# Differential attention on one core: the maxima as rows by DMA, and both softmax sums multiplied before one transpose per quad

## The chip, the cores and the metric

The kernel runs on one core of one Trainium2 chip. The metric is the device time of one launch in microseconds (us); before the change it is 6063.33, the median of three runs (6057.4 to 6066.57).

## The reference

A sandwich of two sublayers on x of 16 batches x 1024 tokens x 256: `x = x + layernorm(attention(layernorm(x)))`, then the same with a mixture of experts. The change is in the attention:

```python
q = rope((x @ Wq).reshape(b, s, 32, 8)); k = rope((x @ Wk).reshape(b, s, 32, 8))   # 2 x 16 heads of width 8
v = (x @ Wv).reshape(b, s, 16, 16)
probs = softmax(q @ k.T * 8 ** -0.5)                 # 32 maps of 1024 x 1024 for each batch
w = probs[even] - lam * probs[odd]                   # the two maps of a head
attn = w @ v
attn = attn * rsqrt(mean(attn ** 2, -1) + 1e-5) * g  # over the 16 values of a head
```

Because the last line divides by the root mean square, attn may carry any factor for each token, if eps is multiplied by the factor's square. The kernel uses that instead of dividing by the softmax sums s1 and s2: with O1 and O2 the unnormalised sums of exp times v, it forms `O1 * s2 - lam * s1 * O2` and adds `(s1 * s2) ** 2 * eps` to the mean square.

## The kernel before

Five stages follow each other: `project` (q, k, v into scratch in device memory), `attend`, `route`, `experts`, `scatter`. Only `attend` changes.

`attend` works on quads: 4 of a batch's 32 maps (2 heads, each with its two maps c = 0 and c = 1). There are 128 quads, taken in a loop of 31 passes of 4 (`BUFS`) with the last 4 unrolled. A quad is 16 groups (`GROUPS`), 8 for each c, one for each tile of 128 keys.

- TensorE (PE), in program order: for each quad 64 `score` matmuls (line 766, keys x 512 queries, into three banks of `ps_e`), the `weighted_sums` of exp against v and 16 columns of ones (line 782, into `ps_o`, two groups late), and, for the next quad, 32 tries (`attempt`, line 795, two matmuls each, into two banks of `ps_m`). A try is one tile of 128 queries against all 1024 keys; it is there only to find the softmax maximum of each query.
- ScalarE (ACT): 64 exponentials for each quad (line 677). A score bank is reused when its exponential is done.
- VectorE (DVE): 32 maxima for each quad (`maximum`, line 691, 128 x 1024 each). Between them stand two 128x32 transposes of the maxima (`turn_maxima`, line 698), two 128x512 transposes of `ps_o` (`turn_sums`, line 703) and one 128x256 transpose of the result (`turn_out`, line 708). Their places are fixed: the transposes of sums stand in groups 1 and 9 (`LAG - 1`, `TILES + LAG - 1`), those of maxima in groups 0 and 8, `turn_out` in group 7 (`HEAD - 1`), each between the two maxima of its group.
- GpSimd (POOL): `split` writes minus the maxima as three bf16 parts (5 small instructions, twice for each quad); `finish` forms the result of a quad.
- SyncE (SP) issues every DMA of the stage in one order, `turn`: rows of maxima c = 0 of the next quad (`load_rows`: four stores to scratch, a wait for them, one load of three rows into `q_stack`, where they stand under the products, so that the score matmul subtracts the maximum), v, the rows c = 1, the 18 loads of the stacks four quads ahead (`load_stacks`, lines 59 and 65), and the four stores of the finished quad, which wait for `turn_out`.

Every engine works in its own order and waits on semaphores; the loop counters are in the wait values. PE waits at group 0 and at group 8 of a quad for the rows of c = 0 and c = 1, and a try waits until the maximum two tries back is done.

Of the kernel before, what the change touches and what calls it, by code (L numbers as in the profile page):

```python
# [22 lines left out]
F32 = mybir.dt.float32  # L23
# [5 lines left out]
P = 128  # L29
# [49 lines left out]
class Build:  # L79
    def __init__(self, nc, io, batches, ctx):  # L80
# [19 lines left out]
        self.max_scr = scratch("max_parts", (b * QKH // 2, PARTS, 2, S), BF16)  # L100
# [354 lines left out]
    def attend(self):  # L455
# [23 lines left out]
        PE_HEAD, ACT_HEAD, DVE_HEAD = 200, 160, 176  # L479
        with ExitStack() as ctx:  # L480
# [7 lines left out]
            v = sb("v", [P, BUFS, 2, 2 * VD * TILES])  # L488
            e = sb("e", [P, E_BUFS, HALF])
            largest, largest_t = sb("largest", [P, 2, 2, BLK]), sb("largest_t", [P, BLK])  # L490
            zeros, negated, rest = sb("zeros", [P, BLK]), sb("negated", [P, BLK]), sb("rest", [P, BLK])
            parts = sb("parts", [P, PARTS, BLK], BF16)
            sums_t = sb("sums_t", [P, 2, BLOCKS, BLK])
            scaled_s1, both = sb("scaled_s1", [P, BLOCKS]), sb("both", [P, BLOCKS])
            normed, attn_t = sb("normed", [P, 2, BLOCKS, VD]), sb("attn_t", [P, BLOCKS // 2, 2, VD])
# [11 lines left out]
            lam_done, lam_step, ones_set, largest_set = sem("lam_done"), sem("lam_step"), sem("ones_set"), sem("largest_set")  # L507
# [9 lines left out]
            ONES = 4  # L517
            SPLIT_STEPS, FINISH_STEPS = 4, 14
# [12 lines left out]
            def _(sp):  # L531
# [18 lines left out]
                def load_v(n, u):  # L550
                    sp.dma_start(v[:, u, :, 0:VD * TILES],
                                 self.v_scr[bass.ds(2 * n, 2)].rearrange("h p m -> p h m")).then_inc(v_loaded[u], 16)

# [32 lines left out]
            def _(pool):  # L586
                nc.gpsimd.memset(v[:, :, :, VD * TILES:], 1.0).then_inc(ones_set, 1)
# [5 lines left out]
                def split(h, base):  # L593

                    pool.wait_ge(max_turned, h + 1)
                    nc.gpsimd.tensor_tensor(negated[:], zeros[:], largest_t[:], ALU.subtract).then_inc(pool_step, 1)  # L596
                    if not (isinstance(h, int) and h == 0):
                        pool.wait_ge(max_stored, 16 * (P // BLK) * h)
# [8 lines left out]
                def finish(n, base):  # L607


                    s1, s2 = sums_t[:, 0, :, VD], sums_t[:, 1, :, VD]  # L610
                    pool.wait_ge(sums_read, 2 * n + 2 + 1)
                    nc.gpsimd.tensor_tensor(scaled_s1[:], s1, neg_lam[:].to_broadcast([P, BLOCKS]), ALU.mult).then_inc(
                        pool_step, 1)
                    nc.gpsimd.tensor_tensor(both[:], s1, s2, ALU.mult).then_inc(pool_step, 1)
                    nc.gpsimd.tensor_tensor(normed[:, 0], sums_t[:, 0, :, 0:VD], s2.unsqueeze(2).to_broadcast([P, BLOCKS, VD]),
                                            ALU.mult).then_inc(pool_step, 1)
                    pool.wait_ge(pool_step, base + 1)
                    nc.gpsimd.tensor_tensor(normed[:, 1], sums_t[:, 1, :, 0:VD],
                                            scaled_s1[:].unsqueeze(2).to_broadcast([P, BLOCKS, VD]),
                                            ALU.mult).then_inc(pool_step, 1)  # L620
                    pool.wait_ge(pool_step, base + 2)
                    nc.gpsimd.tensor_tensor(both[:], both[:], both[:], ALU.mult).then_inc(pool_step, 1)
                    pool.wait_ge(pool_step, base + 4)
                    nc.gpsimd.tensor_tensor(attn[:], normed[:, 0], normed[:, 1], ALU.add).then_inc(pool_step, 1)
                    pool.wait_ge(pool_step, base + 5)
                    nc.gpsimd.tensor_tensor(both[:], both[:], sixteen_eps[:], ALU.mult).then_inc(pool_step, 1)
                    pool.wait_ge(pool_step, base + 6)
                    nc.gpsimd.tensor_tensor(square[:], attn[:], attn[:], ALU.mult).then_inc(pool_step, 1)
                    step = 8
# [17 lines left out]
                def turn(n, rows, base):  # L647
                    if rows:
                        for c in range(2):
                            split(2 * (n + AHEAD) + c, base)  # L650
                            base = base + SPLIT_STEPS
                    finish(n, base)

                for h in range(2 * AHEAD):
                    split(h, SPLIT_STEPS * h)
                pool.wait_ge(lam_done, 1)
                start, steps = 2 * AHEAD * SPLIT_STEPS, 2 * SPLIT_STEPS + FINISH_STEPS
                with hinted(nc, pool, 0, loops) as i:
                    for u in range(BUFS):
                        turn(BUFS * i + u, True, start + steps * (BUFS * i + u))  # L660
                for u in range(BUFS):
                    n = BUFS * loops + u
                    turn(n, u < BUFS - AHEAD, start + steps * n - 2 * SPLIT_STEPS * max(0, u - (BUFS - AHEAD)))

            @block.scalar
            def _(act):
# [3 lines left out]
                with hinted(nc, act, 0, loops + 1, slot=ACT_HEAD) as i:  # L670
                    for u in range(BUFS):
                        n = BUFS * i + u
                        for j in range(HALVES):
                            act.wait_ge(scores_done, HALVES * n + j + 1)
                            if j % QUAD == 0:
                                act.wait_ge(sums_done, GROUPS * n + j // QUAD + 1 - E_GROUPS + E_GROUPS)
                            nc.scalar.activation(e[:, j % E_BUFS], ps_e[:, bank(u, j)], ACT.Exp,  # L677
                                                 scale=SCALE).then_inc(exp_done, 1)

            @block.vector  # L680
            def _(dve):
                nc.vector.memset(largest[:], 0.0).then_inc(largest_set, 1)
                dve.wait_ge(largest_set, 1)
                dve.sem_inc(max_done, 2)
                dve.sem_inc(sums_read, 1)
# [891 lines left out]
```

## Time and profile before

| | before |
|---|---|
| runs, us | 6066.57, 6057.4, 6063.33 |
| profiled execution, us | 6064.04 |
| its span, first to last instruction, us | 6062.2 |
| mean granted TensorE clock | 0.97 of 2.4 GHz |

Durations come from the profiled execution. Its page gives each engine's busy time; a timeline gives instructions in order, with rows of the same line merged and counted; an instruction's duration includes latency that overlaps its successor, so the cost of one in a dense row is the distance of two starts. `attend` fills some 4900 of the 6062 us, from 500 to 5435 us.

### The profile page before, as it was taken

To read this page: it belongs to the slowest core of one execution; us is meant where nothing else is said; L and a number is where in the kernel's file an instruction comes from. 1 tells how busy PE (TensorE), PEld (TensorE's weight loads), DVE (VectorE), ACT (ScalarE), POOL (GpSimd) and SP (SyncE) were. 2 spreads that over 40 slices of the span, in tenths; PEclk is the share of its full clock that TensorE was granted. 3 is DMA by queue.
4 is the path that set the end of the run, shared out by engine and by line. 5 is a ranking of instruction groups with operands and counts; after the bars stand their busy time and mean duration, and the time that the engine had idled before them with its cause. 6 is when DMAs were issued, how large, how long until landed. Compare 5 with 4: busy or idle time off the path is not lost. (4 is left out here: it accounts for less than half of the span.)

```text
span 6062.2 us, 166095 instructions
## 1 busy us (share of the span) xinstructions
PE 5630.7 (93%) x50896; PEld 2015.1 (33%) x50896; DVE 5537.9 (91%) x6200; ACT 4845.1 (80%) x8950; POOL 2006.0 (33%) x3781
## 2 busy tenths in 40 slices
PE   8878999999999999999999999999999999987775
PEld 4542233333333333333333333333233323325424
DVE  7868999999999999999999999999999999967706
ACT  5755888888888888889888888888888888873304
POOL 7981222222222222222222222222222222225406
PEclk9997999999999999999999999999999999998877
DMA  5672222222232222222222222222222222216598
GB/s 178 203 202 49 49 52 52 51 52 52 52 52 51 52 51 52 51 50 52 52 47 51 52 51 48 51 51 51 50 52 52 52 52 51 52 35 199 173 359 272
DMA packets 436840, 493.13 MB, mean 81 GB/s; under 512 B 99283, under 2 KB 298099, under 8 KB 436195
## 3 DMA queue, kind: packets, MB, share of 16 engines
q1 hardware_dynamic: 435171, 483.57, 32.7%
q8 instruction: 457, 7.49, 0.5%
q14 instruction: 188, 1.54, 0.1%
q10 hardware_dynamic: 1024, 0.53, 0.0%
HBM read 360.60 MB, written 123.21 MB: 80 GB/s over the span
## 5 line engine op out<-in xcount | busy, mean ns | idle before, releaser
L677 ACT ACTIVATE at_e<-at_ps_e 128x512 f32<-128x512 f32 x8192 | 4368.8, 595 | 542.5 <-PE at_ps_e L766 373.2
L691 DVE TENSOR_REDUCE at_largest<-at_ps_m 128x1 f32<-128x1024 f32 x4096 | 4671.1, 1202 | 56.2 <-PE at_ps_m L795 53.0
L782 PE MATMUL at_ps_o<-at_e,at_v 128*32 128x256 f32 (+1 forms) x30720 | 2687.1, 422 | 12.3 <-issue 8.2
L795 PE MATMUL at_ps_m<-k_stack,q_stack 48*128 48x512 bf16 x8192 | 2500.1, 385 | 132.7 <-DVE at_largest L691 58.3
L766 PE MATMUL at_ps_e<-q_stack,k_stack 51*128 51x512 bf16 x8192 | 2505.7, 383 | 5.2 <-issue 2.3
L782 PEld LDWEIGHTS at_ps_o<-at_e,at_v 128*32 128x32 f32 x30720 | 845.0, 149 | 1567.3 <-issue 935.0
L766 PEld LDWEIGHTS at_ps_e<-q_stack,k_stack 51*128 51x128 bf16 x8192 | 598.1, 93 | 1678.3 <-ACT at_e L677 1641.0
L596 POOL TENSOR_TENSOR at_negated<-at_zeros,at_largest_t 128x32 f32<-128x32 f32 x256 | 64.7, 253 | 3262.7 <-DVE at_largest_t L698 3262.7
L795 PEld LDWEIGHTS at_ps_m<-k_stack,q_stack 48*128 48x128 bf16 x8192 | 607.6, 93 | 203.5 <-DVE at_largest L691 172.2
L639 POOL TENSOR_TENSOR at_rms<-at_mean_eps,at_minus_half 128x16 f32<-128x16 f32 x128 | 372.7, 2912 | 10.0
L436 PE MATMUL pr_ps_q<-pr_xn_t,pr_w 128*128 128x512 f32 x512 | 232.3, 596 | 2.0 <-issue 1.3
L703 DVE STREAM_TRANSPOSE at_sums_t<-at_ps_o 128x512 f32<-128x512 f32 x256 | 179.2, 700 | 26.3 <-PE at_ps_o L782 26.3
L1040 ACT ACTIVATE ro_x<-ro_ps_y,ro_y_bias,ro_y_rstd 128x256 f32<-128x256 f32 x128 | 61.9, 564 | 165.4 <-POOL ro_y_bias L1002 165.4
L322 ACT CAST pr_parts<-pr_rotated 128x1024 bf16<-128x1024 f32 x64 | 66.8, 1044 | 136.1 <-POOL pr_rotated L266 112.2
L266 POOL TENSOR_TENSOR pr_rotated<-pr_rotated,pr_from_odd 128x1024 f32<-128x1024 f32 x64 | 166.0, 2594 | 29.0 <-DVE pr_from_odd L397 29.0
L633 POOL TENSOR_TENSOR at_square<-at_square 128x128 f32<-128x128 f32 (+3 forms) x512 | 158.7, 310 | 40.1
L271 POOL TENSOR_TENSOR pr_parts<-pr_rest,pr_parts 128x1024 bf16<-128x1024 f32 x64 | 163.4, 2554 | 13.2 <-ACT pr_parts L326 13.2
L382 DVE TENSOR_TENSOR pr_rest<-pr_rotated,pr_parts 128x1024 f32<-128x1024 f32 x64 | 135.0, 2109 | 35.8 <-POOL pr_parts L271 18.6
L1161 PE MATMUL ro_ps_y<-ro_wo,ro_attn 128*128 128x256 f32 x512 | 119.4, 390 | 28.8 <-DMA ro_attn<-attention 20.6
L436 PEld LDWEIGHTS pr_ps_q<-pr_xn_t,pr_w 128*128 128x128 f32 x512 | 98.0, 192 | 98.8 <-issue 94.4
L446 PE MATMUL pr_ps_v<-pr_w,pr_xn_t 128*128 128x256 f32 x512 | 123.4, 385 | 3.8 <-ACT pr_v_out L341 3.8
L1475 ACT ACTIVATE sc_out<-sc_ps,sc_bias,sc_rstd 128x256 f32<-128x256 f32 x128 | 61.7, 563 | 68.0 <-POOL sc_bias L1448 68.0
(130 smaller groups left out, 2856.0 us busy)
## 6 DMA issues: line engine op xcount, KB each, us to landing
k_stack<-k_parts SPq DMA_DIRECT2D x1536, 64.0 KB
q_stack<-q_parts SPq DMA_DIRECT2D x256, 192.0 KB
q_stack<-q_parts SPq DMA_DIRECT2D x256, 128.0 KB
w_first<-in_w SPq DMA_DIRECT2D x32, 1024.0 KB, 11.7
ex_w_second<-in_w SPq DMA_DIRECT2D x32, 1024.0 KB, 12.7
q_parts<-pr_parts SPq DMA_DIRECT2D x96, 256.0 KB, 2.4
k_parts<-pr_parts SPq DMA_DIRECT2D x96, 256.0 KB, 2.8
pr_x_in<-in_x SPq DMA_DIRECT2D x16, 1024.0 KB, 5.8
```

The lines of the kernel that those rows point to most:

```text
L266: nc.gpsimd.tensor_tensor(out, out, from_odd[:, ch % 2], ALU.add if ch % 2 else ALU.subtract).then_inc(add_done, 1)
L271: nc.gpsimd.tensor_tensor(parts[:, ch, 2], rest[:, ch % 2], parts[:, ch, 1], ALU.subtract).then_inc(part3_done, 1)
L382: nc.vector.tensor_tensor(rest[:, ch % 2], rotated[:, ch // 2, ch % 2], parts[:, ch, 0], ALU.subtract).then_inc(rest_done, 1)
L436: last = nc.tensor.matmul(ps_q[:, ch % 2, half * HALF:(half + 1) * HALF], w[:, k, ch // KC, cols], xn_t[:, u, k, half * HALF:(half + 1) * ...
L633: nc.gpsimd.tensor_tensor(square[:, :, 0:width], square[:, :, 0:width], square[:, :, width:2 * width], ALU.add).then_inc(pool_step, 1)
L639: nc.gpsimd.tensor_tensor(rms[:], mean_eps[:], minus_half[:], ALU.pow).then_inc(pool_step, 1)
L677: nc.scalar.activation(e[:, j % E_BUFS], ps_e[:, bank(u, j)], ACT.Exp, scale=SCALE).then_inc(exp_done, 1)
L691: nc.vector.reduce_max(largest[:, u % 2, j // SIDE, j % SIDE:j % SIDE + 1], ps_m[:, j % 2], AX.X).then_inc(max_done, 1)
L703: nc.vector.transpose(sums_t[:, c].rearrange("p b d -> p (b d)"), ps_o[:]).then_inc(sums_read, 1)
L766: nc.tensor.matmul(ps_e[:, bank(u, j)], k_stack[rows, u, pair, c, kt * P:(kt + 1) * P], q_stack[rows, u, pair, c, half * HALF:(half + 1) * ...
L782: last = nc.tensor.matmul(ps_o[32 * tile:32 * tile + 32, columns], v[:, u, tile // 2, kt::TILES], e[:, (QUAD * g + tile) % E_BUFS, columns ...
L795: last = nc.tensor.matmul(ps_m[:, j % 2, half * HALF:(half + 1) * HALF], q_stack[rows, u, pair, c, t * P:(t + 1) * P], k_stack[rows, u, pa ...
```

## The change

1. The maxima (`largest`, [128 queries, 16]) go to scratch as they are, in one DMA (line 549 of the changed kernel), and come back as `largest_t` [16 rows, 128 queries] in a second, element by element (line 554). DVE's two 128x32 transposes are gone. `split` works on 16x128 instead of 128x32. The three parts then go into `q_stack` in six DMAs, one row each (line 559).
2. `ps_o` is copied to `sums` by ACT, once for each c (`copy_sums`), and no longer transposed by DVE. v has ones on both sides, so that for c = 0 a map's rows are O1 | s1 and for c = 1 s2 | O2. POOL multiplies both copies (128x512), which gives O1*s2 | s1*O2.
3. For s1*s2, SP moves one row of sums of each map into `totals`, four DMAs for each c (`move_totals`, line 572), and POOL multiplies these too (128x32).
4. DVE transposes both products at once (128x544, line 746), in group 5 of the next quad (`TURN_SUMS`); `turn_out` moves from group 7 to group 11 (`TURN_OUT`). `finish` has 3 instructions fewer after it.

```diff
+            TURNS_BEFORE = 4
+            ROW_DMAS = PARTS * PAIR
+            DVE_HEAD_PERIODS, TURN_SUMS, TURN_OUT = 12, 5, 11
+            COPY_AT = QUAD * LAG - 1
+            TOTAL_DMAS = 2 * QUAD
...
                 def load_rows(n, u, c):
 
+                    sp.wait_ge(max_done, TRIES * n + SIDE * (c + 1) + 2)
+                    maxima = self.max_scr[bass.ds(2 * n + c, 1)]
+                    sp.dma_start(maxima.rearrange("o q t -> (o q) t"), largest[:, u % 2, c]).then_inc(max_stored, 16)
+                    sp.wait_ge(max_stored, 16 * (2 * n + c + 1))
...
+                        sp.dma_start(largest_t[:], maxima.rearrange("o q t -> (o t) q")).then_inc(max_turned, 16)
                     sp.wait_ge(split_done, 2 * n + c + 1)
-                    maxima = self.max_scr[bass.ds(2 * n + c, 1)]
-                    by_block = maxima.rearrange("o r pair (t g q) -> g (o pair t) r q", t=TILES, q=BLK)
-                    for g in range(P // BLK):
-                        sp.dma_start(by_block[g], parts[BLK * g:BLK * g + SIDE]).then_inc(max_stored, 16)
-                    sp.wait_ge(max_stored, 16 * (P // BLK) * (2 * n + c + 1))
-                    row = SCORE_ROW + PRODUCTS
-                    sp.dma_start(q_stack[row:row + PARTS, u, :, c], maxima.rearrange("o r pair s -> (o r) pair s")).then_inc(
-                        rows_loaded[c][u], 16)
+                    for r in range(PARTS):
+                        row = SCORE_ROW + PRODUCTS + r
+                        for pair in range(PAIR):
+                            sp.dma_start(q_stack[row:row + 1, u, pair, c], parts[TILES * pair:TILES * (pair + 1), r]).then_inc(
+                                rows_loaded[c][u], 16)
...
+                def move_totals(n, c):
+
+                    sp.wait_ge(sums_read, 2 * n + c + 1 + 1)
+                    sp.wait_ge(crossed_done, 2 * n + 2)
+                    for g in range(QUAD):
+                        row = 32 * g + (0 if c else VD)
+                        sp.dma_start(totals[32 * g:32 * g + BLOCKS, c], sums[row:row + 1, c]).then_inc(totals_moved, 16)
...
                         load_v(n + AHEAD, (u + AHEAD) % BUFS)
+                    move_totals(n, 0)
+                    if rows:
                         load_rows(n + AHEAD, (u + AHEAD) % BUFS, 1)
                     if load:
                         sp.wait_ge(scores_done, HALVES * (n + 1))
                         load_stacks(n + BUFS, u)
+                    move_totals(n, 1)
                     store(n, u)
...
                 def finish(n, base):
...
                     pool.wait_ge(sums_read, 2 * n + 2 + 1)
...
+                    nc.gpsimd.tensor_tensor(crossed[:, 0:HALF], sums[:, 0], sums[:, 1], ALU.mult).then_inc(crossed_done, 1)
+                    pool.wait_ge(totals_moved, 16 * TOTAL_DMAS * (n + 1))
+                    nc.gpsimd.tensor_tensor(crossed[:, HALF:], totals[:, 0], totals[:, 1], ALU.mult).then_inc(crossed_done, 1)
+
+                    pool.wait_ge(sums_turned, n + 1)
...
+                def copy_sums(n, c):
+
+                    act.wait_ge(sums_done, GROUPS * n + TILES * (c + 1) + E_GROUPS)
+                    act.wait_ge(crossed_done, 2 * n + 2)
+                    nc.scalar.copy(sums[:, c], ps_o[:]).then_inc(sums_read, 1)
...
+                def turn_sums(n):
+
+                    dve.wait_ge(crossed_done, 2 * (n + 1) + 2)
+                    nc.vector.transpose(crossed_t[:], crossed[:]).then_inc(sums_turned, 1)
...
-                    if g == 0 and rows:
-                        turn_maxima(n, u, 1)
-                    if g == TILES and rows:
-                        turn_maxima(n + 1, u + 1, 0)
-                    if g == LAG - 1 and last_quad:
-                        turn_sums(n - 1, 1)
-                    if g == HEAD - 1 and last_quad:
+                    if g == TURN_SUMS and last_quad:
+                        turn_sums(n - 1)
+                    if g == TURN_OUT and last_quad:
                         turn_out(n - 1, u - 1)
-                    if g == TILES + LAG - 1 and this_quad:
-                        turn_sums(n, 0)
```

The first place is SP's queue in the loop, from the rows of c = 1 to the stores. Before:

```order
L544 DMA max_parts<-at_parts 16x3x32
L545 REGISTER_ALU
L547 DMA q_stack<-max_parts 3x2x1024 [waits at_max_stored]
L568 REGISTER_ALU
L59 ISA [waits at_scores_done]
L59 DMA q_stack<-q_parts 24x4x1024
L59 DMA q_stack<-q_parts 16x4x1024
```
Further on, behind the rest of the stack loads:

```order
L59 DMA q_stack<-q_parts 24x4x1024
L59 DMA q_stack<-q_parts 16x4x1024
L59 DMA q_stack<-q_parts 8x4x1024
L65 DMA k_stack<-k_parts 8x4x1024 x6
L559 ISA [waits at_out_done]
L559 DMA attention<-at_out 2x16x256
L559 ISA
```
After, the first of these places:

```order
L549 DMA maxima<-at_largest 128x16
L550 ISA
L554 DMA at_largest_t<-maxima 16x128x1 [waits at_split_done,at_max_stored]
L559 DMA q_stack<-at_parts 1x8x128 [waits at_split_done]
L559 DMA q_stack<-at_parts 1x8x128 x5
L590 REGISTER_ALU
L59 ISA [waits at_scores_done]
L59 DMA q_stack<-q_parts 24x4x1024
```
and the second:

```order
L59 DMA q_stack<-q_parts 24x4x1024
L59 DMA q_stack<-q_parts 16x4x1024
L59 DMA q_stack<-q_parts 8x4x1024
L65 DMA k_stack<-k_parts 8x4x1024 x6
L568 REGISTER_ALU
L572 DMA at_totals<-at_sums 16x1x32 [waits at_crossed_done,at_sums_read]
L572 DMA at_totals<-at_sums 16x1x32 x3
L579 ISA [waits at_out_done]
L579 DMA attention<-at_out 2x16x256
```
What moved: in front of the stack loads the rows of c = 1 now take a store, a load that waits for it, a wait for POOL's split and six DMAs; and four DMAs of `totals`, on which POOL's second product waits, are queued behind the 18 stack loads and ahead of the stores.

The other engine is DVE, in group 5 of a quad in the changed kernel; `crossed_done` is counted by POOL's two products.

```order
L741 TENSOR_REDUCE at_largest<-at_ps_m 128x1 [waits at_tries_done]
L740 REGISTER_ALU
L741 TENSOR_REDUCE at_largest<-at_ps_m 128x1 [waits at_tries_done]
L745 ISA
L746 STREAM_TRANSPOSE at_crossed_t<-at_crossed 128x544 [waits at_crossed_done]
L740 REGISTER_ALU
```
Before, no transpose stands in group 5; the transpose of sums in group 1 waits for PE alone:

```order
L691 TENSOR_REDUCE at_largest<-at_ps_m 128x1 [waits at_tries_done]
L702 ISA
L703 STREAM_TRANSPOSE at_sums_t<-at_ps_o 128x512 [waits at_sums_done]
L690 REGISTER_ALU
L691 TENSOR_REDUCE at_largest<-at_ps_m 128x1 [waits at_tries_done]
```
What moved: DVE's transpose of sums waits for POOL, which waits for SP's DMAs, and all later maxima are queued behind it.

## Rows read from the trace of the kernel before

**Rows 1.** Page, part 1: busy us (share of the span) x instructions, by engine.
```profile
PE 5630.7 (93%) x50896; PEld 2015.1 (33%) x50896; DVE 5537.9 (91%) x6200; ACT 4845.1 (80%) x8950; POOL 2006.0 (33%) x3781
```

**Rows 2.** Stretches: length; busy PE, PEld, DVE, ACT, POOL (count); clock, DMA, GB/s.
```profile
1500.00:5000.00 3500.00, 3417.66 (x33572) 1091.48 (x33572) 3464.00 (x3377) 3113.78 (x5840) 969.00 (x2276) 1.00 0.26 51
```

**Rows 3.** Timeline, DVE, one quad: start, us, instruction, count.
```profile
3008.94 0.19 DVE L698 STREAM_TRANSPOSE at_largest_t<-at_largest 128x32 f32<-128x32 f32 x1
3009.05 2.31 DVE L691 TENSOR_REDUCE at_largest<-at_ps_m 128x1 f32<-128x1024 f32 x2
3011.29 0.70 DVE L703 STREAM_TRANSPOSE at_sums_t<-at_ps_o 128x512 f32<-128x512 f32 x1
3011.91 13.62 DVE L691 TENSOR_REDUCE at_largest<-at_ps_m 128x1 f32<-128x1024 f32 x12
3025.47 0.42 DVE L708 STREAM_TRANSPOSE at_out<-at_attn_t 128x256 f32<-128x256 f32 x1
3025.81 2.31 DVE L691 TENSOR_REDUCE at_largest<-at_ps_m 128x1 f32<-128x1024 f32 x2
```

**Rows 4.** Timeline, PE, inside the key groups.
```profile
3033.94 0.67 PE L782 MATMUL at_ps_o<-at_e,at_v 128*32 128x256 f32 x8
...
3035.07 0.67 PE L782 MATMUL at_ps_o<-at_e,at_v 128*32 128x256 f32 x8
```

**Rows 5.** Timeline, SP queue, one turn; us is time spent issuing.
```profile
3010.81 1.83 SPq L544 DMA_DIRECT2D max_parts<-at_parts  x4
3013.71 0.79 SPq L547 DMA_DIRECT2D q_stack<-max_parts  x1
3014.79 1.15 SPq L59 DMA_DIRECT2D q_stack<-q_parts  x3
3016.03 2.35 SPq L65 DMA_DIRECT2D k_stack<-k_parts  x6
...
3019.80 2.13 SPq L65 DMA_DIRECT2D k_stack<-k_parts  x6
3026.06 3.25 SPq L559 DMA_DIRECT2D attention<-at_out  x4
3029.93 1.87 SPq L544 DMA_DIRECT2D max_parts<-at_parts  x4
```

**Rows 6.** DMA answer, 3025.9 to 3028.4: packets by size.
```profile
DMA packets 169, 0.28 MB, mean 112 GB/s; under 512 B 35, under 2 KB 35, under 8 KB 168
```

**Rows 7.** DMA answer, 3028.8 to 3031.0.
```profile
DMA packets 153, 0.10 MB, mean 44 GB/s; under 512 B 61, under 2 KB 153, under 8 KB 153
```

**Rows 8.** DMA queue, 3011 to 3013.5: packets, MB, share; issues, us to landing.
```profile
q1 hardware_dynamic: 256, 0.01, 5.7%
...
max_parts<-at_parts SPq DMA_DIRECT2D x4, 3.0 KB, 1.4
```

**Rows 9.** DMA issues, 2537 to 3144: KB each, median us to landing.
```profile
at_v<-v_tiles SPq DMA_DIRECT2D x16, 128.0 KB, 2.1
```

**Rows 10.** Timeline, POOL, one split of the maxima.
```profile
3009.20 0.25 POOL L596 TENSOR_TENSOR at_negated<-at_zeros,at_largest_t 128x32 f32<-128x32 f32 x1 [18.12 <-DVE at_largest_t L698]
...
3010.41 0.25 POOL L605 TENSOR_TENSOR at_parts<-at_rest,at_parts 128x32 bf16<-128x32 f32 x1
```

**Rows 11.** Groups by form, POOL, 2537 to 3144: busy us, mean ns.
```profile
L633 POOL TENSOR_TENSOR at_square<-at_square 128x128 f32<-128x128 f32 x16 | 7.3, 454 | 1.3
```

**Rows 12.** Busy time by stretch, around a halt of PE.
```profile
3140.80:3145.70 4.90, 0.65 (x7) 0.11 (x4) 1.16 (x2) 1.56 (x4) 1.20 (x5) 0.92 0.37 87
3145.70:3151.80 6.10, 6.06 (x33) 1.18 (x36) 4.51 (x5) 2.99 (x6) 0.00 (x0) 0.50 0.11 30
```

**Rows 13.** Timeline, PE, the same place.
```profile
3145.74 0.58 PE L795 MATMUL at_ps_m<-k_stack,q_stack 48*128 48x512 bf16 x1 [4.29 <-issue]
...
3147.27 0.60 PE L766 MATMUL at_ps_e<-q_stack,k_stack 51*128 51x512 bf16 x1
...
3149.26 0.60 PE L766 MATMUL at_ps_e<-q_stack,k_stack 51*128 51x512 bf16 x1
```

More of the change, by code:

```diff
@@ L99, in __init__ @@
         self.v_scr = scratch("v_tiles", (b * HEADS, P, VD * TILES), F32)
-        self.max_scr = scratch("max_parts", (b * QKH // 2, PARTS, 2, S), BF16)
+        self.max_scr = scratch("maxima", (b * QKH // 2, P, 2 * TILES), F32)
         self.attn_scr = scratch("attention", (b * D, S), F32)
@@ L487, in attend @@
             q_stack, k_stack = self.q_stack, self.k_stack
-            v = sb("v", [P, BUFS, 2, 2 * VD * TILES])
+            v = sb("v", [P, BUFS, 2, 3 * VD * TILES])
             e = sb("e", [P, E_BUFS, HALF])
[L490 to L495, printed above, removed]
+            largest, largest_t = sb("largest", [P, 2, 2, SIDE]), sb("largest_t", [SIDE, P])
+            zeros, negated, rest = sb("zeros", [SIDE, P]), sb("negated", [SIDE, P]), sb("rest", [SIDE, P])
+            parts = sb("parts", [SIDE, PARTS, P], BF16)
+            sums, totals = sb("sums", [P, 2, HALF]), sb("totals", [P, 2, BLK])
+            crossed, crossed_t = sb("crossed", [P, HALF + BLK]), sb("crossed_t", [P, HALF + BLK])
+            second, both = sb("second", [P, BLOCKS, VD]), sb("both", [P, BLOCKS])
+            attn_t = sb("attn_t", [P, BLOCKS // 2, 2, VD])
             attn, square = sb("attn", [P, BLOCKS, VD]), sb("square", [P, BLOCKS, VD])
@@ new lines, in load_rows @@
+                    if not (isinstance(n, int) and n == 0 and c == 0):
+                        sp.wait_ge(split_done, 2 * n + c)
+                    with nc.allow_non_contiguous_dma(reason="maxima, one element per query and tile"):
+                        sp.dma_start(largest_t[:], maxima.rearrange("o q t -> (o t) q")).then_inc(max_turned, 16)
+                    sp.wait_ge(split_done, 2 * n + c + 1)
+                    for r in range(PARTS):
[3 more added lines that the diff above has]
+                                rows_loaded[c][u], 16)
@@ L607, in finish @@
                 def finish(n, base):
-                    s1, s2 = sums_t[:, 0, :, VD], sums_t[:, 1, :, VD]
                     pool.wait_ge(sums_read, 2 * n + 2 + 1)
[L612 to L616, printed above, removed]
+                    if not (isinstance(n, int) and n == 0):
+                        pool.wait_ge(sums_turned, n)
@@ L669, in _ @@
                 act.sem_inc(exp_done, SLOTS)
-                with hinted(nc, act, 0, loops + 1, slot=ACT_HEAD) as i:
-                    for u in range(BUFS):
[L672 to L678, printed above, removed]
+                act.sem_inc(sums_read, 1)
@@ new lines, in exponentials @@
+                def exponentials(n, u, first, end):
+                    for j in range(first, end):
+                        act.wait_ge(scores_done, HALVES * n + j + 1)
+                        if j % QUAD == 0:
+                            act.wait_ge(sums_done, GROUPS * n + j // QUAD + 1 - E_GROUPS + E_GROUPS)
+                        nc.scalar.activation(e[:, j % E_BUFS], ps_e[:, bank(u, j)], ACT.Exp,
+                                             scale=SCALE).then_inc(exp_done, 1)
+                def copy_sums(n, c):
+                    act.wait_ge(sums_done, GROUPS * n + TILES * (c + 1) + E_GROUPS)
+                    act.wait_ge(crossed_done, 2 * n + 2)
+                    nc.scalar.copy(sums[:, c], ps_o[:]).then_inc(sums_read, 1)
@@ new lines, in turn @@
+                def turn(n, u, last):
+                    exponentials(n, u, COPY_AT, HALVES // 2 + COPY_AT)
+                    copy_sums(n, 0)
+                    exponentials(n, u, HALVES // 2 + COPY_AT, HALVES)
+                    if not last:
+                        exponentials(n + 1, (u + 1) % BUFS, 0, COPY_AT)
+                    copy_sums(n, 1)
+                exponentials(0, 0, 0, COPY_AT)
+                with hinted(nc, act, 0, loops, slot=ACT_HEAD) as i:
+                    for u in range(BUFS):
+                        turn(BUFS * i + u, u, False)
```

98 lines of the change are left out of this document (49 added, 49 removed).

## The prediction, made before the changed kernel ran

> **What bounds the kernel now.** I read the page's busy shares first: PE 93%, DVE 91%, ACT 80% [rows 1]. Shares mix stages, so next the busy time of a stretch inside `attend`: of 3500 us DVE is busy 3464.0, PE 3417.7, ACT 3113.8, POOL 969.0, at clock 1.00 [rows 2]. ACT runs 64 exponentials for each quad, so 5840 are 91.25 quads, 38.36 us each. Then DVE's timeline: its instructions stand back to back. Twelve maxima take from 3011.91 to 3025.47, 1.13 us each, the transpose of sums holds the engine 0.62 us (3011.29 to 3011.91), that of maxima 0.11, that of the result 0.34 [rows 3]. A quad is 32 x 1.13 + 2 x 0.62 + 2 x 0.11 + 0.34 = 37.96 us of DVE; the rest of the 38.36 are short halts. PE is close behind: inside the groups it needs 3035.07 - 3033.94 = 1.13 us for each try as well [rows 4].
>
> So DVE bounds, and the change relieves it. The view that decides is another: SP's queue. It waits in front of most of its DMAs, and issues 18 stack loads in one piece from 3014.79 to 3021.9, then at 3026.06 the stores of the result [rows 5]. Those stores are runs of 1,024 bytes, so they would count as "under 2 KB" and not "under 512 B". From 3025.9 to 3028.4 both counts are 35: no packet of theirs has moved [rows 6]. From 3028.8 on there are 153 - 61 = 92 [rows 7]. So the queue serves DMAs in order, and what is issued behind the stack loads moves only some 13.8 us after the first of them (3014.79 to about 3028.6).
>
> **The change, part by part.** *DVE.* It loses 2 x 0.11 and 2 x 0.62 and gains one transpose of 128x544: from 0.34 for 256 columns and 0.62 for 512 I take 0.65. That is -0.81 us a quad, 0.8 x 128 = 104 us, if nothing else is late.
>
> *ACT* gets two copies of 128x512. No copy is in the trace; the nearest is the exponential of the same shape, 3113.78 / 5840 = 0.53 us; between nothing and twice that I take 0.55. ACT has (3500 - 3113.8) / 91.25 = 4.2 us idle in a quad [rows 2], which hides 1.1; without that cover it is 1.1 x 128 = 140 us. *POOL* gets two products and loses three small instructions; it is idle 72% of the stretch. I cost both at nothing except where they stand in the chain below.
>
> *The chain through SP.* DVE's transpose of sums in group 5 waits for POOL's second product, this for all eight DMAs of `totals`, and the last four of these are issued behind the rows of c = 1 and the 18 stack loads. DVE is in group 5 after 11 maxima, 12.4 us after the last maximum of the quad before. The chain that starts at that same maximum is far longer, as the terms below show (10.4 + 14.3). Behind DVE's waiting transpose are queued all later maxima, for which PE waits, and with PE ACT. The result is later too, the stores wait for it, and SP begins the next quad's rows behind the stores. So SP's queue and DVE's wait close a ring, and its length is the new time of a quad. Its terms, from the end of `turn_out`:
>
> - A. Wake SP, four stores: 3025.89 to 3026.06, and 3.25 [rows 3, 5]: 3.4 us.
> - B. Rows c = 0. Next issue 0.3. Store of the maxima until landed 1.4 [rows 8]. The load back, 2048 elements of 4 bytes, is not in the trace. Below: 256 small packets took 5.7% of 16 engines in 2.5 us, 8.9 ns each [rows 8], so 128 for each engine are 1.1 on top of 1.4: 2.5. Above: `at_v`, 256 runs of 512 bytes, lands in 2.1 [rows 9], against 1.4 for the 48 runs of a `max_parts` DMA, 0.0034 us a run: 1.4 + 2000 x 0.0034 = 8.2, with bytes that the new load has not. I take 3.6, near the lower end. Split: five instructions, 3009.20 to 3010.66 [rows 10]; with 128 elements in a row one takes 454 ns [rows 11] in place of 250, so 1.46 + 5 x 0.2 + 0.3 for the two wakes = 2.75; unchanged it would be 1.75. Six row DMAs: a stack load is issued every 2.35 / 6 = 0.39, the load of three rows took 0.79 [rows 5]; I take 0.4 each (the source is eight rows, as in the stack load), 2.4 in all, and 5.3 at the upper end. B = 10.45, from 8.15 to 17.95.
> - C. v 0.5 and four `totals` at 0.5 each (four `max_parts` take 1.83 [rows 5]): 2.5.
> - D. Rows c = 1, the same as B: 10.45. Its maxima are done by then.
> - E. First stack load until the `totals` behind it land: 13.8 + 0.5 = 14.3. If they could pass the stack loads: 7.15 of issues, 2.0, 1.4 = 10.55.
> - F. POOL's product and wakes 0.45, DVE's transpose 0.65: 1.1.
> - G. 12 maxima and `turn_out`: 13.62 + 0.42 [rows 3] = 14.05. POOL's `finish` is shorter than that.
> - H. PE's clock. PE halts some 10 us in each ring. The row of before: after 4.29 us idle PE worked at clock 0.50 for 6.1 us [rows 12], which is 1.2 GHz, and a try took 3149.26 - 3147.27 = 1.99 [rows 13] where it takes 1.13 at 2.4 GHz. Three tries so are 2.6 us; I take 2.0, from 0 to 3.4.
>
> Sum: 3.4 + 10.45 + 2.5 + 10.45 + 14.3 + 1.1 + 14.05 + 2.0 = 58.25 us a quad, with B to H at their lower ends 47.9, at their upper ends 74.6. PE's wait for the rows c = 0 lies inside it: they land some 15 us after `turn_out`, PE is ready after 10, and group 5 is reached after some 30, before the 41 at which A to E end.
>
> 124 quads have stack loads: 124 x (58.25 - 38.36) = 2466 us. The last four have none: 58.25 - 14.3 + 3.4 = 47.3, three of them with rows, +27. The two halves of the first quad's rows, one after the other before any score: +10. On the profiled execution's own 6064.04 (span 6062.2), 0.7 above the median of the runs, that gives 8567, so **8570 us**, and as the likeliest case's own range 8000 to 9100.
>
> The Trainium skill, "DMA: Bandwidth & Descriptors", section "Anatomy of one DMA", has a fixed cost of about 2.0 us for each DMA. The rows have 1.4 for the small stores; by the page the two stores of a ring would cost 1.2 us more, an estimate of 150 us more in all, which the sum does not use.
>
> **Rivals.**
> 1. *The totals pass the stack loads.* If a later DMA to other addresses is not held, E is 10.55, the ring 54.5, and the time 6064 + 124 x 16.1 + 37 = 8100. For it: half of the 16 engines may be free, since the DMA share falls after the first loads. Against it: rows 6 and 7.
> 2. *Small pieces are dear.* With 8.2 for each load back the ring is 58.25 + 9.2 = 67.4 and the time 9700; with row DMAs at 0.88 it is 5.8 more on either. For it: 2048 runs is eight times the most that a DMA of this stage has now. Against it: 8.9 ns a packet [rows 8].
> 3. *A load back that is slow by its pattern.* If one engine serves all its elements, where the stores of rows 8 are spread over 16, it takes 2048 x 8.9 ns + 1.4 = 19.6 us; the ring is 58.25 + 2 x 16.0 = 90.25 and the time 12,500. Against it: every DMA of the stage whose landing the rows give is spread. The Trainium skill, "DMA: Bandwidth & Descriptors", section "Rules for kernel authors", puts a transpose by a rearranged access pattern at 19 times the hardware transpose; taken on the 1.4 us of a small DMA that would be 26.6 us and, as an estimate, 14,300 in all. No run shows it yet.
> 4. *Everything at its lower end.* Ring 47.9: 6064 + 124 x 9.5 + 37 = 7280.
> 5. *The relief arrives* (the other side). The `totals` land before DVE reaches group 5, within 12.4 us of the last maximum. It needs B and E together under that, and decides from there: 6064 - 104 = 5960. For it: DVE is the bound now, and each part taken off it is real. Against it: the 18 issues alone take 7.15 us, and the store, the load, the split and six issues in front of them cannot be under 8.
>
> **How the numbers follow.** Forecast 56%, rival 1 14%, rival 2 18%, rival 3 3%, rival 4 5%, rival 5 3%, and 1% that losses and relief cancel. The range 7600 to 9750 leaves out rivals 3 to 5, the ends of the forecast's terms that fall together, and the top of rival 2, near 2 in 10. A measurement of this kernel can tell about 0.2%, 12 us: slower by more 96%, within it 1%, faster 3%.
>
> **What would show it.** In the changed profile: DVE busy near 60% of `attend` and idle in front of line 746, released by POOL; POOL idle in front of its 128x32 product (line 643), released by the DMAs of `totals`; those landing 8 us or more after their issue for c = 1 and about 2 for c = 0; the load back landing in 2.5 to 5; PE idle in front of its tries for about 10 us a quad and for some 5 at group 0, with clock near 0.5 in part of each quad; ACT's copies at 0.55 with no wait behind them. The prediction is wrong if DVE is still busy over 90% of the stage, if the `totals` of c = 1 land in under 3 us, or if a quad is under 48 us.

## The result, and the profile after

| | before | after |
|---|---|---|
| median, us | 6061.75 (6057.4 to 6066.57, 4 runs) | 9620.17 (9560.1 to 9626.76, 4 runs) |
| span of the profiled execution, us | 6062.2 | 9613.3 |
| mean granted TensorE clock | 0.97 | 0.79 |

The ratio is 1.585, with a 95% interval of 1.578 to 1.591: slower by 3558 us, 1050 us above the forecast of 8570. That is inside the range on record, 7600 to 9750, by 130 us, and outside the likeliest case's own range of 8000 to 9100.

First the page's busy shares of the changed kernel, then a stretch inside `attend` (columns as in [rows 2]) and two groups of instructions (busy us, mean ns, idle time before):
```profile
PE 6231.4 (65%) x50896; PEld 1928.8 (20%) x50896; DVE 5561.8 (58%) x5815; ACT 4998.6 (52%) x9206; POOL 2302.5 (24%) x3655
```
```profile
2000.00:8000.00 6000.00, 3789.28 (x33236) 1016.49 (x33232) 3445.20 (x3072) 3189.94 (x5961) 1166.17 (x2160) 0.78 0.19 30
```
```profile
L713 ACT COPY at_sums<-at_ps_o 128x512 f32<-128x512 f32 x180 | 105.0, 583 | 0.0
...
L746 DVE STREAM_TRANSPOSE at_crossed_t<-at_crossed 128x544 f32<-128x544 f32 x90 | 67.1, 745 | 1397.8 <-POOL at_crossed L643 1397.8
```
No engine is the bound any more: DVE's 91% [rows 1] is 58%, and the busiest, PE, is at 65%. ACT has 5961 instructions in the stretch, 180 of them copies, so it holds 5781 / 64 = 90.3 quads of 66.4 us, where a quad took 38.36. The copies came as costed, 583 ns with no wait in front.

Where the time is, the waits of the same stretch say (engine, line, waited for: us, times, longest):
```profile
POOL at_negated L622 <- DMA at_largest_t<-maxima: 2826.0, 180, 20.3
...
POOL at_crossed L643 <- DMA at_totals<-at_sums: 1825.7, 90, 23.8
...
PE at_ps_m L832 <- DVE at_largest L741: 1398.9, 90, 19.8
DVE at_crossed_t L746 <- POOL at_crossed L643: 1397.8, 90, 19.7
DVE at_largest L741 <- PE at_ps_m L832: 1154.5, 666, 10.9
PE at_ps_o L818 <- DMA q_stack<-at_parts: 790.1, 90, 10.3
```
DVE waits in front of its transpose 15.5 us a quad for POOL, POOL for the DMAs of `totals`, and PE's tries wait as long for DVE. PE waits 8.8 us a quad for the rows of the maxima.

One ring in SP's queue, from one group of stores to the next (us is time spent issuing, as in [rows 5]):
```profile
5064.11 3.27 SPq L579 DMA_DIRECT2D attention<-at_out  x4
5068.19 0.39 SPq L549 DMA_DIRECT2D maxima<-at_largest  x1
5071.24 0.33 SPq L554 DMA_DIRECT2D at_largest_t<-maxima  x1
5077.27 4.11 SPq L559 DMA_DIRECT2D q_stack<-at_parts  x6
5081.59 0.40 SPq L563 DMA_DIRECT2D at_v<-v_tiles  x1
5082.18 2.46 SPq L572 DMA_DIRECT2D at_totals<-at_sums  x4
5084.91 0.39 SPq L549 DMA_DIRECT2D maxima<-at_largest  x1
5086.37 0.34 SPq L554 DMA_DIRECT2D at_largest_t<-maxima  x1
5092.43 4.15 SPq L559 DMA_DIRECT2D q_stack<-at_parts  x6
5096.89 1.14 SPq L59 DMA_DIRECT2D q_stack<-q_parts  x3
...
5104.18 2.47 SPq L572 DMA_DIRECT2D at_totals<-at_sums  x4
5129.99 3.26 SPq L579 DMA_DIRECT2D attention<-at_out  x4
```
The same ring on POOL and then on DVE (in brackets the idle time before, and what ended it):
```profile
5074.88 0.44 POOL L622 TENSOR_TENSOR at_negated<-at_zeros,at_largest_t 16x128 f32<-16x128 f32 x1 [19.55 <-DMA at_largest_t<-maxima]
...
5111.13 0.25 POOL L643 TENSOR_TENSOR at_crossed<-at_totals 128x32 f32<-128x32 f32 x1 [17.49 <-DMA at_totals<-at_sums]
```
```profile
5063.51 0.43 DVE L751 STREAM_TRANSPOSE at_out<-at_attn_t 128x256 f32<-128x256 f32 x1
5063.86 10.24 DVE L741 TENSOR_REDUCE at_largest<-at_ps_m 128x1 f32<-128x1024 f32 x9
5084.78 1.22 DVE L741 TENSOR_REDUCE at_largest<-at_ps_m 128x1 f32<-128x1024 f32 x1 [10.68 <-PE at_ps_m L832]
...
5111.41 0.74 DVE L746 STREAM_TRANSPOSE at_crossed_t<-at_crossed 128x544 f32<-128x544 f32 x1 [12.43 <-POOL at_crossed L643]
...
5129.36 0.43 DVE L751 STREAM_TRANSPOSE at_out<-at_attn_t 128x256 f32<-128x256 f32 x1
```
Read them together: stores at 5064.11, rows of c = 0 until 5081.38, `totals`, rows of c = 1 until 5096.58, the 18 stack loads, the last `totals` issued at 5104.18, and POOL gets them at 5111.13. DVE, which had stood still for 12.43 us, goes on, has `turn_out` done 18 us later, and the next stores are issued. From `turn_out` to `turn_out` it is 65.85 us, and each step waits for the one before it.

Where PE halts, its clock falls. The same ring by stretches (columns as in [rows 12]): at full clock, in the halt for the rows of c = 0, and after it.
```profile
5063.90:5074.10 10.20, 8.63 (x92) 2.82 (x88) 10.20 (x10) 9.01 (x17) 0.00 (x0) 1.00 0.17 17
5074.10:5084.80 10.70, 2.14 (x16) 0.53 (x20) 0.02 (x1) 0.40 (x1) 2.13 (x5) 0.50 0.06 14
5084.80:5092.00 7.20, 7.12 (x56) 1.57 (x57) 5.92 (x5) 5.57 (x12) 1.75 (x5) 0.80 0.18 3
```

Two views of single lines: the load back of the maxima, min, median and max of its landing, and the row DMAs, of whose time spent issuing the three numbers are min, median and max in ns.
```profile
DMA to landing us min/median/max: 3.5/3.6/4.7
```
```profile
L559 SPq DMA_DIRECT2D q_stack<-at_parts x1080: 623/632/1357, 2014.2 to 7954.2; - x180
```

### The profile page after: what moved, and what is told of

It is laid out like the page before. It is cut to its first block and busy times, and to the rows that moved or that the text cites. A ratio compares the mean times of both kernels' runs of the same rounds, so it can differ in the third digit from the quotient of the medians.

```text
span 9613.3 us, 166690 instructions
## 1 busy us (share of the span) xinstructions
PE 6231.4 (65%) x50896; PEld 1928.8 (20%) x50896; DVE 5561.8 (58%) x5815; ACT 4998.6 (52%) x9206; POOL 2302.5 (24%) x3655
## 5 line engine op out<-in xcount | busy, mean ns | idle before, releaser
L706 ACT ACTIVATE at_e<-at_ps_e 128x512 f32<-128x512 f32 x8192 | 4430.2, 598 | 3937.0 <-PE at_ps_e L801 3769.4
L741 DVE TENSOR_REDUCE at_largest<-at_ps_m 128x1 f32<-128x1024 f32 x4096 | 4762.3, 1216 | 1639.8 <-PE at_ps_m L832 1634.8
L832 PE MATMUL at_ps_m<-k_stack,q_stack 48*128 48x512 bf16 x8192 | 2805.4, 425 | 1967.6 <-DVE at_largest L741 1931.7
L818 PE MATMUL at_ps_o<-at_e,at_v 128*32 128x256 f32 (+1 forms) x30720 | 2984.4, 465 | 1123.6 <-DMA q_stack<-at_parts 1103.2
L801 PE MATMUL at_ps_e<-q_stack,k_stack 51*128 51x512 bf16 x8192 | 2800.0, 421 | 8.4 <-ACTq L698 1.8
L746 DVE STREAM_TRANSPOSE at_crossed_t<-at_crossed 128x544 f32<-128x544 f32 x128 | 95.4, 745 | 1993.4 <-POOL at_crossed L643 1993.4
L622 POOL TENSOR_TENSOR at_negated<-at_zeros,at_largest_t 16x128 f32<-16x128 f32 x256 | 113.8, 444 | 4032.2 <-DMA at_largest_t<-maxima 4032.2
L832 PEld LDWEIGHTS at_ps_m<-k_stack,q_stack 48*128 48x128 bf16 x8192 | 544.0, 96 | 2080.1 <-DVE at_largest L741 2048.0
L641 POOL TENSOR_TENSOR at_crossed<-at_sums 128x512 f32<-128x512 f32 x128 | 161.9, 1265 | 40.6 <-ACT at_sums L713 40.6
L713 ACT COPY at_sums<-at_ps_o 128x512 f32<-128x512 f32 x256 | 149.3, 583 | 2.7 <-PE at_ps_o L818 2.7
```

Source lines behind the costliest of these rows:

```text
L641: nc.gpsimd.tensor_tensor(crossed[:, 0:HALF], sums[:, 0], sums[:, 1], ALU.mult).then_inc(crossed_done, 1)
L713: nc.scalar.copy(sums[:, c], ps_o[:]).then_inc(sums_read, 1)
L801: nc.tensor.matmul(ps_e[:, bank(u, j)], k_stack[rows, u, pair, c, kt * P:(kt + 1) * P], q_stack[rows, u, pair, c, half * HALF:(half + 1) * ...
L818: last = nc.tensor.matmul(ps_o[32 * tile:32 * tile + 32, columns], v[:, u, tile // 2, first:first + 2 * VD * TILES - kt:TILES], e[:, (QUAD ...
L832: last = nc.tensor.matmul(ps_m[:, j % 2, half * HALF:(half + 1) * HALF], q_stack[rows, u, pair, c, t * P:(t + 1) * P], k_stack[rows, u, pa ...
```

## The experiments

The theory: the time of a quad is the length of the ring through SP's queue, DVE's transpose, `turn_out` and the stores. All times are in us. e1 to e4 and e7 ran once each; beside e1 to e4 before ran at 6056.52, beside e7 its median of 17 runs was 6065.14. The changed kernel's four runs lie within 67 us, and the differences between kernels that are read from single runs are 587 us and more. e5, e6, e8 and e9 are medians of 5 to 12 runs.

**e1, the last `totals` ahead of the stack loads.**
```diff
+                    move_totals(n, 1)
                     if load:
                         sp.wait_ge(scores_done, HALVES * (n + 1))
                         load_stacks(n + BUFS, u)
-                    move_totals(n, 1)
```

> Only the order of SP's queue changes: the four totals of c = 1 are issued ahead of the 18 stack loads. Theory (the ring through SP's queue, with the totals held behind the stack loads): in the changed kernel's trace the terms of a quad are A 3.5, B 12.7, C 3.4, D 12.1, 0.3, E 17.0, F 1.0, G 16.5 = 66.5 us. E becomes the issue of four DMAs 2.7, landing and wake 2.1, so the quad 66.5 - 17.0 + 4.8 = 54.3 us and the time 9613 - 124 x 12.2 = 8100 us. Rival 1 (the order of the queue is not what holds DVE; PE waits for the rows of the maxima, and the totals are late beside it): under 2 us a quad are won, the time stays above 9350. Rival 2 (POOL's two products and ACT's copies set DVE's wait): nothing changes, 9600.

Measured: 7949.63 in one run; this one move gives back 1670 us, where the theory had 1500 and the rivals less than 270. In its trace:
```profile
4013.51 3.50 SPq L572 DMA_DIRECT2D at_totals<-at_sums  x4
4017.34 1.13 SPq L59 DMA_DIRECT2D q_stack<-q_parts  x3
```
```profile
4018.45 0.74 DVE L746 STREAM_TRANSPOSE at_crossed_t<-at_crossed 128x544 f32<-128x544 f32 x1 [3.83 <-POOL at_crossed L643]
```
In this turn DVE goes on 1.1 us after the first stack load is issued, where in the turn shown above it went on 14.5 us after it. The ring is 53.1 us in the mean, 54.3 by the theory. It is still one: SP reaches the rows only after `turn_out`.

**e7, the same 18 stack loads with a sixteenth of their bytes** (an argument `width` of 64 in `load_stacks`).
```diff
-            queue.dma_start(q_stack[row:row + rows].rearrange("r pair c s -> r (pair c) s"),
-                            heads_q[0:rows]).then_inc(loaded, 16)
+            queue.dma_start(q_stack[row:row + rows].rearrange("r pair c s -> r (pair c) s")[:, :, 0:width],
+                            heads_q[0:rows][:, :, 0:width]).then_inc(loaded, 16)
```

> The changed kernel, but the 18 stack loads of a quad inside attend move 64 of every 1024 columns (the rest of the stacks keeps old data, so the output is not the reference's); they are as many, with as many pieces, and are issued at the same places. Theory (the totals are held by the queue's data, 15 us of it): E falls from 17.0 to the issues 7.4, four totals 2.5, landing and wake 2.0 = 11.9 us, the quad by 5.1, the time to 9613 - 124 x 5.1 = 8980. Rival (E is SP's issuing and a slow landing, the data are beside the point): above 9500.

Measured: 8869.22, near the theory's 8980. From the first stack load to POOL's second product it now takes 11.0 us (mean of 124 turns) in place of 17.0, and the whole ring is shorter by the same 6.0:
```profile
5041.86 1.58 SPq L59 DMA_DIRECT2D q_stack<-q_parts  x3
...
5049.61 2.47 SPq L572 DMA_DIRECT2D at_totals<-at_sums  x4
```
```profile
5053.30 0.25 POOL L643 TENSOR_TENSOR at_crossed<-at_totals 128x32 f32<-128x32 f32 x1 [14.67 <-DMA at_totals<-at_sums]
```
The `totals` are issued at the same distance as in the changed kernel (7.4 us in the mean of both) and wait for the data in front of them. Of the 17.0 us, 11.0 are issuing and one small DMA's way, 6.0 the bytes.

The packets in the changed kernel's trace say what waits. The four `totals` of c = 1 move in 64 packets of 128 bytes. In each of 124 turns 32 of them have started by 3.3 us after the first issue (3.26 to 3.44), while packets of the stack loads, 2048 bytes each, still move. The last starts after 7.9 us in the mean (4.5 to 11.5), always 0.1 to 0.4 us after the last packet of the stack loads. So at least half of the data passes the stack loads, but never all of it, and POOL's product waits for all. Rival 1's reason, that half of the 16 DMA engines may be free, fits this, but its shorter E does not follow: 17.0 us, not 10.55.

**e4, the load back of the maxima done twice**, the second after a wait for the first.
```diff
+                        sp.dma_start(largest_t[:], maxima.rearrange("o q t -> (o t) q")).then_inc(max_again, 16)
+                        sp.wait_ge(max_again, 16 * (2 * n + c + 1))
                         sp.dma_start(largest_t[:], maxima.rearrange("o q t -> (o t) q")).then_inc(max_turned, 16)
```

> The load back of the maxima (2048 elements of 4 bytes) is done twice, the second waiting for the first; everything else is the changed kernel. Theory (a ring: every us in SP's chain is a us of the quad, for c = 0 as for c = 1): 2 x 3.8 us more a quad, 9613 + 126 x 7.6 = 10570 us. Rival (only one of the two halves is on the path, the other lies beside work of PE or DVE): 3.8 a quad, 10090 us. Rival 2 (neither, the wait is for the stack loads' data alone): 9620 us.

Measured: 10515.97, 896 us more than the changed kernel, for two extra loads of some 3.6 us in a ring: 896 / 124 = 7.2. The theory's time was 10570, that of a ring with one half alone 10090: the rows of both c lie on the ring, at full price. The two loads of c = 0 in this kernel:
```profile
5051.69 0.32 SPq L555 DMA_DIRECT2D at_largest_t<-maxima  x1
5055.28 0.32 SPq L557 DMA_DIRECT2D at_largest_t<-maxima  x1
```

**e3 and e2, each part of the change alone**: e3 is before with part 1 (maxima through scratch, `turn_maxima` gone, six row DMAs); e2 is the changed kernel with part 1 taken back (`turn_maxima` in groups 0 and 8, four stores and one load).
```diff
-                        turn_maxima(n, u, 1)
-                        turn_maxima(n + 1, u + 1, 0)
```
(these two lines are in e2 and not in e3)

> The part of the change on the maxima alone; the sums are transposed by DVE as before, no totals are moved. Theory: rows of c = 1 take 12.1 us from the last maximum, so the stack loads are drained at 1 + 12.1 + 0.3 + 15.2 = 28.6 us after PE's group 0 (18.6 + in the kernel before); the stores of the result are queued behind them, then come four stores 2.9, the store of the maxima 1.4, the load 3.7, the split 2.4, row DMAs 4.1 and landing 1.5. Rows of c = 0 land at about 44 us, where PE wants them at 37.9: the quad is 44, the time 6064 + 124 x 5.5 = 6750 us. Rival (a queue with time left: SP has 38 us a quad and its DMAs are all off the path): 6040 to 6100 us, DVE wins 0.2 us a quad.

> The part of the change on the sums alone, with the order of SP's queue as in the change; the maxima are transposed by DVE and go to the rows as before. Theory: DVE reaches group 5 12.4 us after a quad's last maximum; the totals land after 5.9 (last maximum to first stack load, in the trace of before) + 17.0 (E) = 22.9. The quad is 22.9 + 1.0 + 16.5 + 9 maxima 10.2 = 50.6 us, the time 6064 + 124 x 12.2 = 7580 us. Rival (the 2048-element load and the six row DMAs are what makes the change slow; the sums part by itself only relieves DVE): 5960 to 6100 us.

Measured: e3 6643.85 (theory 6750), e2 7897.28 (theory 7580). Together they would be 587 + 1841 = 2428 us; the whole change costs 3560. The rows of one c hold SP's queue for 3.7 us before (3010.81 to 3014.50 [rows 5]) and for 12 or more after, some 17 us a quad. Alone they have cover, since no transpose of sums then waits for a DMA, and 4.7 of them get out (587 / 124), at the place where e3's theory had them, in front of PE. From 1500 to 5000, in 81 quads, 3.2 us each:
```profile
PE at_ps_o L780 <- DMA q_stack<-at_parts: 259.1, 56, 9.4
```
In e2's ring most of them count: (9620 - 7897) / 124 = 13.9 a quad. e2 missed its theory by 317 us: its quad is 52.9 us in the mean and not 50.6. The totals are used 16.8 us after the first stack load, as expected, but from `turn_out` to that load it is 18.6 us, where the theory had 10.2 + 5.9 = 16.1; it counted 9 maxima there, and DVE's timeline has 10, which is 1.1 of the 2.5. In e3 SP's queue also shows a store caught behind the stack loads:
```profile
4011.21 3.19 SPq L566 DMA_DIRECT2D attention<-at_out  x4
4014.70 0.40 SPq L544 DMA_DIRECT2D maxima<-at_largest  x1
4024.20 0.33 SPq L549 DMA_DIRECT2D at_largest_t<-maxima  x1
```
The load waits for the store to land: 9.50 us in this turn. Over 125 turns it is 6.2 us in the mean, from 1.9 to 11.6; for the store of c = 1, with no stores of the result in front, 1.7. e3's quads are of many lengths too, from 37.7 to 49.9 us.

**e5 to e9, is there gain in the sums part?** e5 is e2 with the last `totals` ahead of the stack loads; e6 is e5 with `turn_out` one group earlier; e8 is e6 with the head slots of before; e9 is e6 with both transposes one group earlier.
```diff
-            DVE_HEAD_PERIODS, TURN_SUMS, TURN_OUT = 12, 5, 11     # e5
+            DVE_HEAD_PERIODS, TURN_SUMS, TURN_OUT = 12, 5, 10     # e6, e8
+            DVE_HEAD_PERIODS, TURN_SUMS, TURN_OUT = 12, 4, 9      # e9
-        PE_HEAD, ACT_HEAD, DVE_HEAD = 200, 144, 204               # e5, e6, e9
+        PE_HEAD, ACT_HEAD, DVE_HEAD = 200, 160, 176               # e8
```

> The part on the sums alone, as in the kernel with the sums part only, but with the totals of c = 1 issued ahead of the 18 stack loads. Theory: the totals land 5.9 + 2.7 + 2.1 = 10.7 us after a quad's last maximum, DVE is in group 5 after 12.4, so nothing holds it; the stores of the result and the rows of c = 0 end about 1 us before PE wants them. DVE loses 2 x 0.62 of transposes and gains one of 0.67: -0.57 us a quad, 73 us, and ACT's copies and POOL's products stay hidden: 5990 us, between 5980 and 6060. Rival 1 (ACT's copies stand in front of exponentials that PE waits for, three score banks do not cover 0.55 us): PE loses up to 2 x 0.3 us a quad and the relief is gone, 6060 to 6140. Rival 2 (the two ends of SP's chain meet all the same, a quad of 39 to 41 us): 6140 to 6400.

> As the kernel before this one in the list, with turn_out in group 10 in place of 11, so that SP stores the result and starts the rows of c = 0 one group (2.3 us) earlier. POOL's part after DVE's transpose of sums takes 7.8 us and DVE 10 maxima, 11.3 us, so turn_out does not wait. Theory: the same 5990 if the slack of the rows is there already, and up to 1 us a quad less than the other if it is not. Rival: turn_out then waits for POOL, the time is above the other's by 0.5 us a quad or more.

> The sums part with its totals ahead of the stack loads and turn_out in group 10, as in e6_sums_out10, but with the head slots of ACT's and DVE's loops as in the kernel before (160 and 176 in place of 144 and 204). Open is why the 0.41 us a quad that e6 gains in its quiet quads (37.50 against 37.91) don't reach the time. Theory 1: the first quads of a pass are longer because of where the loops' first instructions stand; if the slots of before were the better ones, DVE's idle time in 1500 to 5000 falls from 68 towards the 35 us of before, and the time is 6064 + 20 - 0.41 x 124 = about 6035 or less. Rival: the slots don't matter, PE is late there for what it does itself (it has less than 0.5 us to spare in a quad); then the time stays at 6070 to 6085.

> The same kernel as e6_sums_out10 with its slots, but DVE's transpose of the products in group 4 and turn_out in group 9, one group earlier each, so that SP comes to the next quad's rows 2.3 us earlier. Theory 1: if the long quads of e6 (38.4 to 38.9 beside 37.5) come from rows that land just in time for PE, they shrink and the time falls to 6030 to 6065. Rival: the long quads have to do with the loops' back edges alone; the time is 6070 to 6085 as before. If the totals of c = 1 land too late for group 4 (they are issued some 3 us ahead of it), DVE waits for POOL again by 0.5 to 2 us a quad, and the time is above 6130.

| kernel | median, us (range) | ratio to before, 95% |
|---|---|---|
| e5 | 6271.27 (6254.24 to 6289.77) | 1.0346, 1.0328 to 1.0363 |
| e6 | 6077.65 (6066.36 to 6090.68) | 1.0022, 1.0014 to 1.0031 |
| e8 | 6078.01 (6074.12 to 6082.25) | 1.0023, 1.0014 to 1.0032 |
| e9 | 6174.01 (6168.82 to 6177.82) | 1.0182, 1.0168 to 1.0196 |

e5 missed its 5990. DVE no longer waits for POOL, but `turn_out` in group 11 lets SP begin the rows so late that PE waits for them, in 1500 to 5000:
```profile
PE at_ps_o L823 <- DMA q_stack<-max_parts: 81.6, 69, 2.7
```
That is 0.9 us a quad of the 1.6 by which e5 is longer than e6; the rest was not followed up. One group earlier (e6) takes 194 us off. The time is then 12.5 us above that of before, a loss of 0.2% (interval 0.14 to 0.31%). In e6 DVE is relieved, by 0.41 us a quad where the sum had 0.57; one quiet quad between two `turn_out`:
```profile
3033.89 0.44 DVE L750 STREAM_TRANSPOSE at_out<-at_attn_t 128x256 f32<-128x256 f32 x1
3034.24 13.64 DVE L733 TENSOR_REDUCE at_largest<-at_ps_m 128x1 f32<-128x1024 f32 x12
3047.79 0.20 DVE L740 STREAM_TRANSPOSE at_largest_t<-at_largest 128x32 f32<-128x32 f32 x1
...
3071.38 0.43 DVE L750 STREAM_TRANSPOSE at_out<-at_attn_t 128x256 f32<-128x256 f32 x1
```
It is 3071.38 - 3033.89 = 37.49 us, against 37.90 in the quiet quads of before. But over 1500 to 5000 DVE waits for PE more. Its wait in e6, then in before:
```profile
DVE at_largest L733 <- PE at_ps_m L837: 68.3, 57, 8.3
```
```profile
DVE at_largest L691 <- PE at_ps_m L795: 35.4, 29, 5.5
```
33 us more of waiting eat most of the 0.41 x 91 = 37 us that 91 quads win. The waits stand in two quads of each pass of four, where in before one is longer than the quiet ones. The mean of all quads of the stretch is 38.40 us in e6 and 38.36 in before; the few us that the waits leave open are not explained. At one place in each pass PE's tries halt for nothing that the profile shows: 23 times, 46.2 us in e6 and 31.7 in before. The head slots don't explain it: with those of before (e8) the time is the same. e9 makes DVE wait again, for POOL's product:
```profile
DVE at_crossed_t L745 <- POOL at_crossed L636: 59.4, 90, 2.0
```
e9's wait for POOL is 0.7 us a quad, of the 0.8 by which it is longer than e6. So no version beats the kernel before. Why PE's halts once in a pass are longer in e6 stays open. Issuing the `totals` from another engine's queue than SP's was not tried.

## Why the prediction was right, and where its sizes were off

The mechanism was right, by its own signs: the ring, DVE idle in front of line 746, POOL in front of line 643, PE's halts with the clock at 0.50, the clock of the stage at 0.78. One sign came out a little short: the last of the four `totals` of c = 1 lands 7.6 us after its issue in the mean (4.0 to 11.6), where 8 or more was expected; those of c = 0 land after 1.9. The sum was 8.25 us a quad too short, and the time left the likeliest range; that it stayed inside the range on record is in part luck, since the range reached to 9750 for rival 2's sake, a slow load back that did not come. Its terms against the mean of 123 turns of the changed kernel, read from its trace in the same way as the ring shown above:

| term | forecast | measured |
|---|---|---|
| A wake, stores | 3.4 | 3.5 |
| B rows c = 0 | 10.45 | 12.7 |
| C v, `totals` | 2.5 | 3.4 |
| D rows c = 1 | 10.45 | 12.1 |
| E stack loads until `totals` are used | 14.3 | 17.0, and 0.3 ahead of it |
| F product, transpose | 1.1 | 1.0 |
| G, H maxima, clock | 16.05 | 16.5 |
| ring | 58.25 | 66.5 |

- *B and D, +3.9.* The mis-sized step is "I take 0.4 each" for the six row DMAs. They take 0.63 to issue and follow each other every 0.69, so six are 4.1 and not 2.4: 3.5 of the 3.9. The nearest row was not the stack load but the load of three rows at 0.79, which the prediction kept for its upper end. The store of c = 0 took 2.1 until the load was issued and not 1.4, which with the gaps in front of both stores makes +0.9; the loads with POOL's wake are +0.2, the two splits, 2.4 and not 2.75, -0.7.
- The load back, the least certain term, was right: 3.6. That was luck, since 3.6 was picked between 2.5 and 8.2 and followed from neither. *Rival 3* falls. The Trainium skill, "DMA: Bandwidth & Descriptors", section "Rules for kernel authors", states 19 times against the hardware transpose; the prediction applied it to a small DMA's 1.4 us, an estimate of 26.6 us, and this trace has 3.6. No run has a hardware transpose, so the ratio itself is not tested here.
- The fixed cost of about 2.0 us for each DMA, which the prediction took from the Trainium skill, "DMA: Bandwidth & Descriptors", section "Anatomy of one DMA", is stated there for DMAs that GpSimd issues; these are SyncE's. Here the two stores of the maxima land after 1.8 us in the mean of 256 (median 1.65, 1.42 to 3.20), between the 1.4 of the rows and the 2.0 of that page.
- *E, +2.7.* Its 13.8 was read from one turn. From the first stack load's issue to its last packet the two kernels take the same, 15.2 us in the mean of 124 turns of before and after, but 12.3 to 18.7 by turn; the turn that I read was shorter than the mean. The `totals` also land and are picked up 1.8 after that, and not 0.5.
- *C, +0.9.* A DMA of `totals` takes 0.58 to issue, every 0.62, and not 0.5.
- *Rival 2* is half right: small pieces are dear to issue (0.69 a row against its 0.88), not to move. Its 9700 is near the measured time by luck: it came from 8.2 us for each load back, and that is 3.6.
- *Rival 1* fails as a time by e7: E is 17.0, although half of the `totals` data and more does pass the stack loads. The prediction's "the queue serves DMAs in order" holds for the last packet, which is the one that POOL waits for. *Rival 4* falls by B, D and E. As its terms stand, B's lower end is 0.3 + 1.4 + 2.5 + 1.75 + 2.4 = 8.35 and not 8.15, which makes rival 4 7330 and changes nothing else. *Rival 5*, the relief, arrives only in e6's quiet quads, and by 0.41 us, with both `totals` ahead of the stack loads and the rows left as they were.
- PE's halts were forecast at 10 and 5 us a quad; they are 15.5 (1398.9 us of waiting for DVE in 90 quads) and 8.8. That changes little, since both lie inside the ring.

8.25 us more a quad in 124 quads are 1020 of the 1050 us that the forecast was short.

## What to carry to other kernels

Before giving a queue one more DMA that an engine waits for, walk the queue in program order: what stands in front of it is the price, and if that engine's later work feeds the queue again, every microsecond of the ring is paid in full (e4: 7.2 us for two loads of some 3.6), while the busiest engine works 65% of the time. Read a term that comes from a queue's draining from many turns, not from one. Two changes that share such a ring are not to be costed apart: 587 and 1841 us alone were 3560 together.

## What the hardware showed that was not expected

- Issuing costs by shape, by the distance of two starts: 0.39 us for one DMA of 24 to 8 rows of stacks, 0.62 for one row to sixteen (`totals`), 0.69 for eight rows into one partition (`q_stack`). The store of 128 x 16 maxima, which stands alone, spends 0.39 issuing.
- A load of 2048 single elements from scratch lands in 3.6 us, twice a small DMA's time, and less than the six issues behind it take.
- A store of 8 KB, behind 18 stack loads and the stores of the result, needs 6.2 us in the mean (1.9 to 11.6) from its issue to the load that waits for it (e3), where that of c = 1 needs 1.7.
- Of four small DMAs issued behind 18 large ones in one queue, half of the packets start within 3.5 us of the first issue, with the large ones still moving; the last starts 4.5 to 11.5 us after it, when the large ones have ended (124 turns). The order of a queue held here for the last packet and not for each.
